# A CIN tower whose first group is loaded and multiplied in two parts

## What is computed

```
e  = stack of tbl_f[ids[:, f]] for f in 0..38            # (512, 39, 16)
X1 = einsum('hjk,bjd,bkd->bhd', W0, e, e)  + b0          # H = 128
X2 = einsum('hjk,bjd,bkd->bhd', W1, e, X1) + b1
X3 = einsum('hjk,bjd,bkd->bhd', W2, e, X2) + b2
z  = concat(X1.sum(2), X2.sum(2), X3.sum(2))             # (512, 384)
h  = relu(concat(z, dense) @ W_top1 + b_top1)            # 512
h  = relu(h @ W_top2 + b_top2)                           # 256
y  = h @ W_top3
```

## Time and profile before

| | us |
|---|---|
| median of 3 runs | 663.0 (662.79 to 663.69) |
| the profiled execution | 663.66 |
| its span | 661.8 |
| busy: PE / DVE / ACT / POOL | 631.5 / 544.8 / 510.3 / 370.6 |
| mean granted clock of TensorE, share of full | 0.995 |
| chain that ended last: share of PE | 84% |

### The profile page before, as it was taken

The page is one execution under the profiler, slowest core; times in us unless marked ns, Lnnn a source line. Parts: engine busy times, 40 slices in busy tenths (PEclk is TensorE's granted clock), DMA queues, the critical chain, the costliest instruction groups (busy, mean ns, idle before and its releaser), DMA issues.

```text
span 661.8 us, 12303 instructions
## 1 busy us (share of the span) xinstructions
PE 631.5 (95%) x2578; PEld 470.5 (71%) x2578; DVE 544.8 (82%) x1527; ACT 510.3 (77%) x1746; POOL 370.6 (56%) x312
## 2 busy tenths in 40 slices
PE   0689999999999999999999999999999999999998
PEld 0247777777777777777777777777777777786574
DVE  0348788898989898989988898989898989989692
ACT  2228878878887888787888878887888787897494
POOL 6888656575657676665667575656675222223000
PEclk9899999999999999999999999999999999999999
DMA  7356787767778776767776767778777665657100
GB/s 226 47 109 151 128 180 136 162 129 161 135 155 162 155 150 151 142 145 136 149 155 137 161 129 159 135 154 162 155 152 150 144 144 129 165 125 211 33 0 1
DMA packets 62282, 91.18 MB, mean 138 GB/s; under 512 B 34711, under 2 KB 38724, under 8 KB 62007
## 3 DMA queue, kind: packets, MB, share of 16 engines
q0 software_dynamic: 14192, 51.02, 42.9%
q1 hardware_dynamic: 48070, 39.95, 22.2%
HBM read 10.69 MB, written 1.28 MB: 18 GB/s over the span
## 4 chain that ended last, share of the span: by engine, by line
PE 84%; POOL 6%; DMA 5%; issue 2%; DVE 1%; ACT 1%; SPq 1%; DVEq 0%; POOLq 0%
PE t_bank L509 21%; PE t_bank L510 20%; PE t_bank L511 20%; PE x_bank L467 7%; POOL emb L377 6%; PE small_bank L494 5%; PE x_bank L463 1%; PE x_bank L462 1%; PE x_bank L465 1%; PE t_bank L578 1%; DMA rep<-emb_scratch 1%; PE t_bank L609 1%; DMA emb_scratch<-emb 1%; DMA rep<-rep 1%; DMA shared<-rep 1%
## 5 line engine op out<-in xcount | busy, mean ns | idle before, releaser
L686 ACT ACTIVATE prod<-t_bank,x0t 128x128 f32<-128x128 f32 x1472 | 415.2, 381 | 70.9 <-PE t_bank L511 68.4
L810 DVE SCALAR_TENSOR_TENSOR prod<-t_bank,x0t,prod 128x128 f32<-128x128 f32 x1024 | 286.1, 339 | 49.9 <-PE t_bank L511 49.7
L509 PE MATMUL t_bank<-w_hi,x_hi 128*128 128x512 f32 (+1 forms) x640 | 288.9, 451 | 1.0 <-DVE x_lo L799 0.8
L510 PE MATMUL t_bank<-w_lo,x_hi 128*128 128x512 f32 (+1 forms) x640 | 247.1, 386 | 0.0
L511 PE MATMUL t_bank<-w_hi,x_lo 128*128 128x512 f32 (+1 forms) x640 | 246.7, 385 | 0.0
L377 POOL DMA_INDIRECT emb<-in_table,idx x160 | 212.1, 1325 | 48.5 <-issue 47.6
L387 POOL TENSOR_TENSOR diag<-x0t,mask 128x320 f32<-128x320 f32 x64 | 86.7, 1355 | 185.1 <-PE small_bank L494 111.5
L509 PEld LDWEIGHTS t_bank<-w_hi,x_hi 128*128 128x128 f32 x640 | 120.2, 188 | 45.7 <-issue 16.6
L510 PEld LDWEIGHTS t_bank<-w_lo,x_hi 128*128 128x128 f32 x640 | 120.5, 188 | 37.8 <-issue 14.4
L511 PEld LDWEIGHTS t_bank<-w_hi,x_lo 128*128 128x128 f32 x640 | 120.1, 188 | 23.8
L842 DVE TENSOR_TENSOR prod<-prod 128x768 f32<-128x768 f32 x189 | 113.4, 600 | 0.2
(11 more groups left out here) (104 smaller groups left out, 381.6 us busy)
## 6 DMA issues: line engine op xcount, KB each, us to landing
prod<-prod POOLq DMA_DIRECT2D x63, 768.0 KB, 6.7
shared<-rep SPq DMA_DIRECT2D x96, 234.0 KB
shared<-rep SPq DMA_DIRECT2D x48, 78.0 KB
emb<-in_table,idx POOLq DMA_INDIRECT x160, 5.4
G<-in_w SPq DMA_DIRECT2D x1, 2496.0 KB
rep<-rep SPq DMA_DIRECT2D x28, 78.0 KB
rep<-emb_scratch SPq DMA_DIRECT2D x20, 78.0 KB
prod<-in_w SPq DMA_DIRECT2D x1, 1536.0 KB, 8.1
```

The lines of the kernel that those rows point to most:

```text
L509: pe.matmul(acc, hi, w1_hi[:, cols], start=True, stop=False)
L510: pe.matmul(acc, hi, w1_lo[:, cols], start=False, stop=False)
L686: last = act.activation(prod[:, s, SLOT[c] + u, :], t_bank[c % T_BANKS][:, u * H:(u + 1) * H], ACT.Copy, scale=x0t[:, s, j:j + 1])
L810: last = dve.scalar_tensor_tensor(unit, t_bank[c % T_BANKS][:, u * H:(u + 1) * H], x0t[:, s, j:j + 1], unit, ALU.mult, ALU.add)
```

## The change

- **Group 0 in two parts** of 256 columns. Each part has its own ids, index, five gathers of 126 or 124 rows (`gather_part`), store (two DMAs), load (four, half as wide) and factors. Part 0's pairs are formed and multiplied before group 0's chunks into `t_bank[3]`; then the chunks of tiles 0 and 1 run on its x1. Part 1's transposes stand at position 8, its forms at 7 to 13, its products at 10 to 16, its x1 in tile 1 ahead of chunk 7. Second factors of the parts have six places of their own in `prod`; ScalarE's queue issues part 0's second, fourth and sixth.
- **Group 1** is gathered and stored behind them; its x0 is asked for at position 20 instead of 8, and its forms and products stand at 24 to 33 and 27 to 36, all products unsplit. Its x1 is finished behind chunk 7 of tile 3 instead of chunk 5, its x1_lo at 38 instead of 36.
- **Group 2**: GpSimd gathers it in tiles 0 and 1 of group 0 instead of ahead of group 0. ScalarE waits for the gathers ahead of chunk 9 of tile 2 and issues the store from its own queue. SyncE loads the rows fourfold from DRAM behind group 1's sixth second factor.
- **w1** is loaded and split in four pieces, three of them ahead of the chunks and the fourth behind the forms of part 0; b1 is loaded once and copied three times by ScalarE; small tables that only the end needs are loaded in group 13.

The core of the diff:

```diff
+            for part in range(PARTS):
+                load_part_ids(part)
+            load_w1(0)
+            sp.dma_start(pair_a_raw, pair_a).then_inc(pair_w_loaded, 16)
+            sp.dma_start(pair_b_raw, pair_b).then_inc(pair_w_loaded, 16)
+            load_w1(1)
             sp.dma_start(ids_all[:, :], ids).then_inc(ids_loaded, 16)
             sp.dma_start(table_at[:, :], starts).then_inc(ids_loaded, 16)
...
+            def factors_of_part(part):
+
+                sp.wait_ge((early_x0_loaded, x0_loaded)[part], 16 * X0_LOADS)
+                cols = part_cols(part)
...
+                if part > 0:
+                    sp.wait_ge(early_pair_ready, BLOCKS)
+                for b in range(1, BLOCKS):
+                    if part > 0 or b % 2 == 1:
+                        sp.dma_start(part_second_at(part, b), rep[b:b + PAIRS, 0, cols]).then_inc(part_second[b - 1], 16)
+                    if part > 0 and b == FIRST_STORE_BEHIND:
+                        store_rows(1, 1)
+
+            store_part(0)
+            load_w1(3)
+            load_part(0)
+            factors_of_part(0)
+            store_part(1)
+            load_part(1)
+            factors_of_part(1)
+
+            load_x0(1, 1, range(0, REP_ROWS, F))
+            factors(1, 1)
+            sp.wait_ge(x0t_mm, 1)
+            load_x0(2, 0, range(0, REP_ROWS, F))
...
-            for g in range(AHEAD):
-                index(g, g)
-                for i in range(GATHERS):
-                    gather(i, g)
-            pool.wait_ge(small_loaded, 16 * SMALL_LOADS)
+            for part in range(PARTS):
+                gather_part(part)
+            pool.wait_ge(ids_loaded, 16 * 2)
+            index(1, 1)
+            for i in range(GATHERS):
+                gather(i, 1)
...
+                        if first and (s, c) == STORE_ROWS_AT:
+                            act.wait_ge(emb_stored, 16)
+                            act.wait_ge(gathered[0], 16 * GATHERS)
+                            act.dma_start(emb_dram[2 * ROW_PARTS:3 * ROW_PARTS, :], emb[:, 0, :]).then_inc(emb_stored, 16)
+                        if first and (s, c) == PART_X1_AT:
+                            last_part_x1_hi()
...
+FIRST_FORM_AT = [24, 25, 27, 28, 30, 31, 33]
+FIRST_PAIR_AT = [27, 28, 30, 31, 33, 34, 36]
+FIRST_X1_AT = (3, 7)
+STORE_ROWS_AT = (2, 9)
+FIRST_LO_AT = 38
```

More of the change, by code:

```diff
@@ L66 @@
 EARLY_COLS = B - 2 * TB
-SMALL_LOADS = 7 + TILES_PER_GROUP
+HEAD_LOADS = 2
+LOOP_LOADS = 2
+TAIL_LOADS = 4
 WARM_UP = (5, 3, 0, 2)
@@ L271, in _, with load_part_ids, load_w1 @@
         def _(sp):
+            def load_part_ids(part):
+                begin, n = PART_BEGIN[part], PART_SIZE[part]
+                for fold in range(FOLDS):
+                    sp.dma_start(part_ids[fold * n:(fold + 1) * n, part, :],
+                                 ids[begin:begin + n, fold * PART_GATHERS:(fold + 1) * PART_GATHERS]).then_inc(part_ids_loaded[part], 16)
+            def load_w1(i):
+                cols = slice(W1_PIECES[i][0] * H, W1_PIECES[i][1] * H)
+                sp.dma_start(w1_raw[:, cols], w1[:, cols]).then_inc(w1_loaded[i], 16)
@@ L326, in factors, with store_part @@
                         load_x0(g + 1, 1 - half, [0])
-            for g in range(2):
-                store_rows(g, g)
-                load_x0(g, g, range(0, REP_ROWS, F))
-                if g == 0:
-                    factors(0, 0)
-            with sp.Fori(1, GROUPS - 2, 2) as odd:
-                for g, half in ((odd, 1), (odd + 1, 0)):
+            def store_part(part):
+                sp.wait_ge(part_gathered[part], 16 * PART_GATHERS)
+                begin, n = PART_BEGIN[part], PART_SIZE[part]
+                row = PART_GATHERS * D
+                for fold in range(FOLDS):
+                    sp.dma_start(emb_dram[begin:begin + n, fold * row:(fold + 1) * row],
+                                 part_emb[fold * n:(fold + 1) * n, part, :]).then_inc(part_stored[part], 16)
@@ new lines, in load_part @@
+            def load_part(part):
+                sp.wait_ge(part_stored[part], 16 * FOLDS)
+                src = emb_rows[part * PART_ROWS:(part + 1) * PART_ROWS, :].rearrange("(b f) d -> f b d", f=F)
+                for row in range(0, REP_ROWS, F):
+                    n = min(F, REP_ROWS - row)
+                    sp.dma_start(rep[row:row + n, 0, part_cols(part)].rearrange("f (b d) -> f b d", d=D),
+                                 src[0:n]).then_inc((early_x0_loaded, x0_loaded)[part], 16)
@@ L336, in _ @@
+            store_part(0)
[9 more added lines that the diff above has]
+            load_x0(2, 0, range(0, REP_ROWS, F))
+            with sp.Fori(2, GROUPS - 2, 2) as even:
+                for g, half in ((even, 0), (even + 1, 1)):
                     factors(g, half, then_x0=True)
@@ L423, in group @@
                         fold((s - 1) % TILES_PER_GROUP)
-                    if gathers and s < INDEX_TILE:
+                    if first:
+                        for i in range(*FIRST_GATHERS[s]):
+                            gather(i, half if s < FIRST_INDEX_TILE else 1 - half)
+                    elif gathers and s < INDEX_TILE:
                         for i in range(GATHERS_EARLY, GATHERS):
                             gather(i, half)
-                    if early and s >= INDEX_TILE:
+                    if early and not first and s >= INDEX_TILE:
                         for i in range(3 * (s - INDEX_TILE), 3 * (s - INDEX_TILE) + 3):
@@ L503, in t_chunk @@
                     pe.wait_ge(x0t_ready, then_x0t * TILES_PER_GROUP)
+                if first_tile and c in W1_CHUNKS:
+                    pe.wait_ge(w_split_lo, W1_CHUNKS.index(c) + 1)
                 if not (first_tile and c < T_BANKS):
```

338 lines of the change are left out of this document (245 added, 93 removed).

## The result

| | before | after |
|---|---|---|
| median of 6 runs, us | 663.46 (662.79 to 664.59) | 660.43 (659.60 to 661.96) |
| ratio, 95% interval | | 0.9957 [0.9939, 0.9975] |
| profiled execution / its span, us | 663.66 / 661.8 | 661.96 / 660.1 |
| mean granted clock | 0.995 | 0.992 |
| first chunk / group 1 / group 2 start, us | 45.67 / 79.67 / 116.42 | 35.10 / 77.70 / 114.71 |

One of the six runs of each kernel was disturbed (719.15 us before, 2224.87 after) and is left out of the ranges and of the interval; without it the medians are 663.23 and 660.35.

The account below looks back on a forecast made before the run. TensorE was taken as the bound, so only group 2's start could gain: 31.3 + 37.25 + 2.1 + 35.7 = 106.35 against 116.42, -10.1 us, giving 663.0 - 10.1, rounded to 653.0; own range 649.5 to 656.5, with rivals 648.8 to 658.5.

Parts of the forecast that it names:

- the sum: Group 2's start: 31.3 + 37.25 + 2.1 + 35.7 = 106.35 against 116.42, so -10.1 us.
- Part 4: Rows of part 1, group 1 and group 2 come in time, all waits hidden; GpSimd's index addition loses about 0.5 us.
- Part 5: Group 1 takes 35.7 us instead of 36.75, so -1.05, with tile 1 folded ten us ahead of its use.
- Part 1: Group 0's first half: x0 at 21.2, first chunk at 31.3 instead of 45.67; cold clock costed at nothing.
- rival (b): Head: w1's loads share DMA engines with part 0; start at 34.5 or cold TensorE; 656 to 658.5, chance 0.12.
- Part 2: Work coming back into group 0 among the chunks, from products and transposes: 37.25 us instead of 33.55.
- Part 3: Edge between groups 0 and 1: TensorE waits 2.1 us instead of 0.45, bounds 1.0 and 3.5.
- Rival (a): Group 1's rows come late, index addition held behind w1_lo; TensorE waits at position 20; 656 to 657, chance 0.20.
- rival (d): Tile 2: ScalarE's wait for group 2's rows stops TensorE, making it slower than before; 664 to 667, chance 0.04.
- Rival (e): Groups 0 to 2: start moves, but another engine's pace returns the time as TensorE waits; 661.7 to 664.3, chance 0.03.

Follow-up runs that it names:

- the small folds: The changed kernel with the three folds of group 0 cut to one of twelve blocks, part of the sums left out: 656.77, 0.9908.
- the six edits: Six versions of the changed kernel with whole folds, four single edits of positions, fold order, edge or load and two combinations: 659.73, 660.24, 662.63, 662.29, 661.48, 663.32.
- the edge edit: The changed kernel with group 1's last product at 35, x1 behind chunk 5 of tile 3 and x1_lo at 36, as before: 662.63, 0.9991.
- the first experiment: The changed kernel with extra warm-up matmuls, WARM_UP (8, 5, 0, 2) instead of (5, 3, 0, 2): 661.32, 0.9984.
- the first combination: The changed kernel with warm-ups (8, 5, 0, 2), tile 1's fold behind tile 2's gathers, group 1's first two blocks formed at 22 and 23: 661.48, 0.9977.
- the early forms: The changed kernel with group 1's first two blocks formed at positions 22 and 23 instead of 24 and 25: 659.73, 0.9963.
- the late fold: The changed kernel with tile 1's fold issued behind tile 2's gathers instead of ahead of them: 660.24, 0.9969.
- the single load: The changed kernel with group 2's rows loaded once from DRAM and copied three times, instead of loaded fourfold: 662.29, 0.9996.
- the split folds: The changed kernel, edge untouched, with each fold of group 0 as three DMAs of 256 KB with a gather between them: 657.47, 0.9909.
- the three pieces in a row: The changed kernel with each fold of group 0 as three 256 KB DMAs in a row ahead of the next tile's gathers: 660.45, 0.9986.

## Why the prediction was wrong

Group 2 began at 114.71, 8.36 us later than the 106.35 of the sum: 3.8 at the start, 3.25 in group 0 with its edge, 1.31 in group 1.

**Part 4, the step that failed.** It asked when group 1's x0 comes, and the sum has no term for the way from that x0 to the seven blocks; of group 2's load it says "issued near 60 and done by 66" and "Hidden". Both were thus put at nothing, with durations (about 2 us for a second factor, some 6 for the loads) from the head before, where no fold ran. What the runs showed in its place: the copies meet tile 1's fold, the fourth second factor takes 8 us, and the load is issued at 67.30 and takes 8.34. Part 5 even named the fold, "near 59, ten us ahead of its use", as a gain for its own consumer, and never as traffic. The trace of before already held the missing number. A fold lands only after 7.1 to 7.7 us, and a store of group 2's 78 KB, issued 1.6 us behind one, let the load that waits for it go 6.7 us later, where the earlier trace rows have 2.19 (GpSimd's and SyncE's timelines of the kernel before):

```profile
57.69 1.00 POOL L399 DMA_DIRECT2D prod<-prod  x1
...
59.33 0.31 SPq L292 DMA_DIRECT2D emb_scratch<-emb  x1
...
66.05 0.36 SPq L300 DMA_DIRECT2D rep<-emb_scratch  x1
```

In the change's profile the fold's direct cost is the one wait of 1.59 us. It is more where the start is earlier, 3.6 us of waits with the extra warm-up, and by the medians the small folds took off 3.7. The fold moves TensorE's first wait to wherever the next needed transfer lies, which is why none of the six edits gained anything over the change that their intervals can show.

That the small folds with the edge edit came to 654.02, 1.0 from the forecast, is partly luck. The sum had counted 2.1 us of waiting at the edge, and the edge edit takes that wait away. Like for like are the small folds alone, 656.77: their group 2 began at 110.49, still 4.1 us behind the sum, 1.7 of it at the first chunk (32.97), 1.2 in group 0 with its edge and 1.3 in group 1. These are the terms of parts 1, 2 and 3 below.

**Part 1.** x0 of part 0 at 21.69 (21.2) and the last form done at 29.80 (29.0) were close, so the load of 4.3 us between 17.41 and 21.69 bore out the 4.4 taken. (The 3.7 that the prediction worked out from the Trainium skill, "DMA: Bandwidth & Descriptors", section "Anatomy of one DMA", rests on a fit for DMAs of GpSimd's queue, and this load is SyncE's; the trace does not agree with it by 0.6 us.) The cold clock was put "at nothing": the trace shows a granted clock of 0.73 and 0.59 from 25 to 35, the lower of the two levels for most of it, after waits of TensorE of 3.08, 1.92 and 0.60 us; from the last form to the first chunk it took 5.3 us instead of 2.3. The prediction had the price (2.5) but no chance on it outside rival (b). It does not set the time, by the first experiment.

**Part 2.** 18.5 us from the first chunk to position 20, where 16.6 were reckoned. 1.03 of the difference is a wait that the sum lacked: the prediction asked when part 1's forms come, not its x1_lo, behind ScalarE's x1 and x1_hi. About 0.9 remains without a name.

**Part 3.** The edge: 1.84 against 2.1 forecast. Right in size, but it carried a second cost: in the trace of after the granted clock is 0.52 from 80 to 82, and in that of the small folds 0.60 from 74 to 78, some 1.5 us lost in group 1 (37.01 against 35.43 with small folds and the edge edit). That is why **Part 5** read 37.01 instead of 35.7. The kernel without the wait at the edge has 1.00 there. The drop is not certain behind such a wait: the clock stayed at 1.00 in seven of the twelve profiles that show one.

**Part 4, GpSimd.** The index addition took 0.22 us, less than the 0.5 taken; but the lock fell on the instruction next to it. The gather of 4.51 us ends 1.2 us behind VectorE's piece (22.03 against 20.88). The Trainium skill, "SBUF — State Buffer", section "SBUF: two separate sides", confines this lock, for a VectorE operation with two SBUF inputs, to a GpSimd operation that reads SBUF. In the trace it is an indirect DMA that was held, by 3.2 us; whether its reading of the indices is what the page means, no run here shows. Rival (a) was right on the hold, if not on the instruction, and on the lateness (tenth gather 3.3 us late, its price 656 to 657). Its supposed symptom, a wait at position 20 for x0, did not come: SyncE asked for the factors at 49.63, and TensorE's wait at 53.61 is for x1_lo. The load did get later into the stretch of the fold, but how much of that is due to the hold stays open.

**ScalarE's wait** (rival (d)) was covered, as forecast: its store was issued at 60.47, with no wait of TensorE behind it. **Rival (e)**, that the same time comes back because another engine paces groups 0 to 2, came nearest: the cause was not an engine but the DMA traffic, and some seven tenths of the gain came back, not all.

## What to carry to other kernels

When work is moved so that small copies on the critical chain run at the time of a large DMA, take their latency from a stretch where such a DMA is in flight, not from a quiet one; and list for each transfer of the chain the bytes issued just ahead of it on any queue. If removing a wait only moves it, look for the one resource behind all of them before tuning positions. A large DMA that is not urgent can be issued in pieces with other work between them; here that took 3 us off, and the same pieces in a row nothing.

## What the runs showed of the hardware

- **A small DMA behind a large one on another queue.** SyncE's load of group 2 issued in 6.5 to 10.9 us with 768 KB of fold ahead on GpSimd's queue, whether as one DMA or three in a row, and in 2.6 to 5.1 with the fold spread out or small. The Trainium skill, "DMA: Bandwidth & Descriptors", section "Queues, rings and completion order", has each DMA engine take turns between the queues packet by packet; a delay that did not change when the same bytes were cut into three DMAs agrees with that. Why 234 KB then take 8 us is not worked out here.
- **Instruction fetch.** With four or eight VectorE instructions more ahead of the loop the kernel took 34 to 37 us more than the one before: six waits of about 6.5 us, one per pass, with 30 or 31 instead of 4 instruction packets. That the waits are for instructions is read from these packets. Five matmuls more ahead of TensorE's loop, or six DMAs more on GpSimd's, had no such effect. Why these lengths and not others is open.
- **Clock.** A wait of 1.84 to 1.86 us at the edge was followed by 3 to 4 us at a granted clock near 0.6 in five profiles (the change, the extra warm-up, the small folds without and with it, the first combination). A wait of 1.84 to 1.89 us was followed by no drop in seven others (the early forms, the late fold, the single load, the split folds, the three pieces in a row, and both with w1_lo in smaller pieces). The 4.05 us at 88.50 with the edge edit were followed by 0.50, the lower level, from 90 to 94.
- **Spread.** With whole folds most changed kernels vary more from run to run than the kernel before in the same series (657.8 to 662.5 for the early forms against 661.4 to 663.7), and with tile 1's fold small less (654.2 to 655.8). That the fold and the factors meet at slightly different moments would explain it, but was not tested, and the kernel before alone went from 661.7 to 668.1 in one series.
